# A mixture of experts with the slot lists made by products of one-hot matrices and the rows gathered for each tile

## The chip, the cores and the metric

The kernel runs on one core of one Trainium2 chip. The time is the device time of one execution in microseconds; a median over runs is quoted, and a profile is one execution of its own. PE is the matrix engine, DVE the vector engine, ACT the scalar engine, POOL the general engine, SP the engine that only issues transfers.

## The reference

Two pre-norm blocks on `x` of 2 x 1024 tokens with 256 features, all in float32: ALiBi attention with 32 heads, a mixture of experts, an RWKV-7 time mixing, and a feed-forward switched between two experts. The change lies in the second, which is

```
xf = layernorm(x)
gates = softmax(xf @ router_w.T)                  # 8 experts
topv, topi = top_k(gates, 2)
masked = zeros_like(gates) with topv at topi;  masked /= masked.sum() + 1e-20
for e in range(8):
    routed += (silu(xf @ wg[e]) * (xf @ wu[e]) @ wd[e]) * masked[:, e]   # hidden 176
shared = silu(xf @ sg) * (xf @ su) @ sd                                  # hidden 352
x = x + routed + shared
```

## The kernel before

The program is a row of blocks; at the end of a block all engines meet. Tokens lie 128 to a partition tile, 16 tiles (`TILES`), and four tiles make a chunk of 512 tokens (`TB`, four chunks, `NB`). A token chooses two experts, so there are 4096 choices (`CHOICES`). The kernel doesn't run each expert over all tokens: it sorts the choices by expert into slots, 128 slots to a tile, each expert's part rounded up to whole tiles. This gives at most 39 tiles (`SLOT_TILES`), and all 39 are worked on.

The blocks around the change, in order:

- `attention_phase` (L486). In the last but one of its units SP also issues one transfer of 5 MB that fills the slot table in memory with blank rows (`slot_rows`, `blank`), and waits for it at the end of the phase (L721 to L724, L761).
- `project_attention` (L764), beside which SP loads all weights of the mixture, and `layernorm_stats` (L66).
- `normalise_rows` (L902). DVE normalises the 16 tiles into `rows`, which holds each row twice (once for each choice) with two more words for the choice's number and its gate; POOL makes the second copy (L923). PE turns the tiles and ACT takes them into `xt`.
- `route_and_share` (L946). PE forms the router's logits (L1012) and turns them to token order (L1016). DVE has a chain of some 30 small operations, each waiting for the one before (`c.link`): softmax, the two picks, the mask, the gates; PE sums the mask over tokens (L1024, L1025), and DVE makes from it the slot of each choice, `at32` (L1116), and the expert of each tile, `tile_expert` (L1121). POOL then scatters the rows to the slot table with 32 indirect transfers of 128 rows (L1133) and waits until all have landed. Beside this the shared expert runs in 12 steps, three for a chunk: `gate_and_up(i)` on PE (L997), the silu on ACT (L1045), the product `share(i)` on DVE (L1071), `down(i)` on PE (L1006); after three steps DVE adds the chunk to `x` (`take(n)`, L1076).
- `routed_experts` (L1138). PE first loads the 39 expert numbers into registers, one by one (`value_load`). Then for each tile j: SP loads the slots (L1174; five buffers, `RING_T`), PE turns them (L1196), gate and up product with that expert's weights, addressed by the register (L1204), silu on ACT (L1251), product on DVE (L1276), PE turns it (L1213), down product (L1221), DVE weighs it with the gate (L1284), POOL scatters the result to `moe_chosen` by the choice's number (L1308). A slot buffer is loaded again when its tile's scatter has landed, for the gate and the number are read from it. At the end SP loads the results back by chunk, two for each token, and DVE adds them to `x` (L1298) and takes the statistics for the next normalisation (L63).

SP's queue holds the slot loads and, after the sixth, 16 loads of weights for the time mixing.

## Time and profile before

| | |
|---|---|
| median of 3 runs | 1524.67 us (1517.23 to 1526.18) |
| profiled execution, its time | 1534.31 us |
| its span | 1532.5 us |
| busy PE, DVE, ACT, POOL | 1253.8, 866.6, 565.9, 246.1 us |
| mean granted clock of TensorE | 0.924 of full speed |
| moved by DMA | 56.71 MB, mean 37 GB/s |

The span is the time from the first to the last instruction; the time of an execution holds a little more. A time in a timeline counts from the span's start. "Idle before" is how long the engine had nothing to do ahead of that work, and the name behind the arrow is what ended it: another engine's instruction, a DMA, "issue" when nothing that the profile shows was waited for, "remote" when the signal came from nothing recorded on this core. A clock of 1.00 is 2.4 GHz and 0.50 is 1.2 GHz.

### The profile page before, as it was taken

To read this page: it belongs to the slowest core of one execution; us is meant where nothing else is said; L and a number is where in the kernel's file an instruction comes from. 1 tells how busy PE (TensorE), PEld (TensorE's weight loads), DVE (VectorE), ACT (ScalarE), POOL (GpSimd) and SP (SyncE) were. 2 spreads that over 40 slices of the span, in tenths; PEclk is the share of its full clock that TensorE was granted. 3 is DMA by queue.
4 is the path that set the end of the run, shared out by engine and by line. 5 is a ranking of instruction groups with operands and counts; after the bars stand their busy time and mean duration, and the time that the engine had idled before them with its cause. 6 is when DMAs were issued, how large, how long until landed. Compare 5 with 4: busy or idle time off the path is not lost. (4 is left out here: it accounts for less than half of the span.)

```text
span 1532.5 us, 32535 instructions
## 1 busy us (share of the span) xinstructions
PE 1253.8 (82%) x12936; PEld 710.8 (46%) x12968; DVE 866.6 (57%) x1704; ACT 565.9 (37%) x846; POOL 246.1 (16%) x454
## 2 busy tenths in 40 slices
PE   5779999999999997947366662877599999976998
PEld 3423333333333335524244441333288888864665
DVE  5477888888888844401011226777667766665122
ACT  2417777777777773300122221533221112102211
POOL 3310000001001004360012220122232112100000
PEclk9959999999999998888689995999899999998999
DMA  3401112211211324020122223000020000000000
GB/s 110 67 3 25 26 26 39 32 25 29 42 24 25 93 70 142 20 91 18 50 71 61 66 63 110 0 1 0 1 72 3 4 4 4 4 2 0 14 14 28
DMA packets 42589, 56.71 MB, mean 37 GB/s; under 512 B 13067, under 2 KB 32235, under 8 KB 42123
## 3 DMA queue, kind: packets, MB, share of 16 engines
q1 hardware_dynamic: 38299, 44.67, 12.5%
q0 software_dynamic: 3408, 9.34, 1.7%
q8 instruction: 86, 1.41, 0.4%
q10 hardware_dynamic: 768, 1.05, 0.2%
q14 instruction: 28, 0.23, 0.1%
HBM read 28.73 MB, written 16.59 MB: 30 GB/s over the span
## 5 line engine op out<-in xcount | busy, mean ns | idle before, releaser
L664 DVE TENSOR_REDUCE at_block_max<-at_p_ring 128x4 f32<-128x512 f32 x576 | 367.6, 685 | 75.9 <-PE at_p_ring L570 41.6
L641 ACT ACTIVATE at_probs<-at_p_score,abias 128x1024 f32<-128x1024 f32 (+2 forms) x320 | 318.9, 1029 | 122.6 <-PE at_p_score L600 68.4
L570 PE MATMUL at_p_ring<-kt,qt 64*128 64x128 bf16 (+3 forms) x1152 | 186.9, 284 | 18.5 <-PEq L730 7.3
L615 PE MATMUL at_p_out<-at_probs,at_vs 128*32 128x512 f32 (+3 forms) x1536 | 164.2, 500 | 0.4 <-ACT at_probs L641 0.4
L594 PE MATMUL at_p_score<-qt,kt 64*128 64x512 bf16 (+3 forms) x768 | 145.9, 331 | 5.7 <-ACT at_probs L641 4.8
L570 PEld LDWEIGHTS at_p_ring<-kt,qt 64*128 64x128 bf16 x1152 | 69.9, 96 | 130.2 <-DVE at_block_max L664 86.3
L1276 DVE TENSOR_TENSOR ex_hidden<-ex_p_gu,ex_act 128x176 f32<-128x176 f32 x39 | 13.3, 341 | 140.2 <-ACT ex_act L1251 140.2
L1196 PE MATMUL ex_p_turn<-ident,ex_slot 128*128 128x128 f32 x78 | 17.6, 313 | 76.3 <-DMA ex_slot<-moe_slots 49.3
L594 PEld LDWEIGHTS at_p_score<-qt,kt 64*128 64x128 bf16 x768 | 38.3, 94 | 86.2 <-ACT at_probs L641 55.2
L707 POOL TENSOR_TENSOR at_shift<-shift,at_row_max 128x16 f32<-128x16 f32 x32 | 7.1, 220 | 422.8 <-DVE at_row_max L670 422.8
L1308 POOL DMA_INDIRECT moe_chosen<-ex_y,ex_slot x39 | 37.2, 955 | 196.2 <-DVE ex_y L1284 195.6
L1970 ACT COPY rc_ta<-rc_bank 128x256 f32<-128x256 f32 x32 | 10.3, 375 | 149.2 <-PE rc_bank L1741 149.2
L1388 DVE SCALAR_TENSOR_TENSOR tm_xm<-tm_xx,vec,xt_mix 128x512 f32<-128x512 f32 x48 | 44.5, 974 | 35.4 <-PE tm_p_full L1498 30.0
L2210 DVE SCALAR_TENSOR_TENSOR x<-ff_p_out,branch,x 128x256 f32<-128x256 f32 x32 | 13.3, 477 | 87.2 <-PE ff_p_out L2166 87.2
L600 PE MATMUL at_p_score<-anticausal,ident 128*128 128x128 bf16 (+1 forms) x384 | 62.3, 244 | 0.0
L2175 PE MATMUL ff_p_in<-xt_ffn,w_in 128*128 128x512 f32 x128 | 61.3, 607 | 1.2 <-PEq L2100 1.2
L1204 PE MATMUL ex_p_gu<-w_routed,ex_xs 128*128 x156 | 60.2, 514 | 0.1
L2166 PE MATMUL ff_p_out<-w_back,ff_hidden 128*128 128x256 f32 x256 | 59.8, 379 | 0.0
L1245 ACT COPY ex_xs<-ex_p_turn 128x256 f32<-128x256 f32 x39 | 14.5, 372 | 117.8 <-PE ex_p_turn L1196 117.8
L2166 PEld LDWEIGHTS ff_p_out<-w_back,ff_hidden 128*128 128x128 f32 x256 | 48.6, 190 | 18.6 <-issue 13.4
L2190 ACT ACTIVATE ff_hidden<-ff_p_in,b_in 128x512 f32<-128x512 f32 x32 | 22.0, 688 | 86.2 <-PE ff_p_in L2175 86.2
L615 PEld LDWEIGHTS at_p_out<-at_probs,at_vs 128*32 128x32 f32 x1536 | 30.2, 108 | 45.6 <-issue 38.1
(301 smaller groups left out, 2220.2 us busy)
## 6 DMA issues: line engine op xcount, KB each, us to landing
qt<-qparts SPq DMA_DIRECT2D x96, 64.0 KB, 2.4
kt<-kparts SPq DMA_DIRECT2D x96, 64.0 KB, 2.4
moe_slots<-in_blank_dram SPq DMA_DIRECT2D x1, 5031.0 KB, 19.3
ex_slot<-moe_slots SPq DMA_DIRECT2D x39, 129.0 KB, 2.1
ex_back<-moe_chosen SPq DMA_DIRECT2D x8, 512.0 KB, 5.0
w_routed<-in_w_routed_dram SPq DMA_DIRECT2D x1, 2816.0 KB
x<-in_x_dram SPq DMA_DIRECT2D x4, 512.0 KB, 8.4
out_dram<-x SPq DMA_DIRECT2D x4, 512.0 KB, 2.9
```

Source lines behind the costliest of these rows:

```text
L570: mm = pe.matmul(bank[:, col:col + nb * P], qt[nxt][h * ROWS:(h + 1) * ROWS, pair, t * P:(t + 1) * P], kt[nxt][h * ROWS:(h + 1) * ROWS, pa ...
L594: mm = pe.matmul(score[:, h, i * w:(i + 1) * w], kt[now][h * ROWS:(h + 1) * ROWS, pair, key * P:(key + 1) * P], qt[now][h * ROWS:(h + 1) * ...
L600: mm = pe.matmul(over, ident16[:, :], anticausal16[:, 0:len(pairs), :], start=False, stop=True, skip_group_check=True)
L615: mm = pe.matmul(p_out[32 * h:32 * h + 32, left(k):QC], vs[(now - e[2]) % BUFS][:, key, h, :], probs[g % PROBS][:, h % 2, at:at + w], star ...
L641: act.activation(probs[g % PROBS][:, :, 0:len(pairs) * w], p_score[g % 2][:, :, 0:len(pairs) * w], ACT.Exp, bias=abias[:, c * TPB + key:c ...
L664: dve.tensor_reduce(dst, src, AX.X, ALU.max).then_inc(s["fill_used"], 1)
L1204: mm = pe.matmul(p_gu[j % 2][:, 0:2 * HIDDEN], xs[j % 2][:, h, :], w_routed[:, h, ds(expert[j], 1), :].rearrange("p a c -> p (a c)"), star ...
L1308: pool.indirect_dma_start(chosen_out[:, :], bass.IndirectOffsetOnAxis(ap=slot[i][:, AT_ID:AT_ID + 1].bitcast(I32), axis=0), y[i][:, :], No ...
L1388: ins = dve.scalar_tensor_tensor(xm[i % 2][:, h, :], xx[:, h, :], v_("x_" + MIXES[i], h), xt[:, h, ds(m, 1), 1:].rearrange("p n c -> p (n ...
L2166: mm = pe.matmul(p_out[e][:, t, :], hidden[m % 2][:, t * P:(t + 1) * P], w_out[:, m, :], start=m % FT == 0 and t % 2 == 0, stop=m % FT == ...
L2175: mm = pe.matmul(p_in[m % 2][:, :], w_in[:, h, m * P:(m + 1) * P], xt[:, h, ds(n, 1), 1:].rearrange("p n c -> p (n c)"), start=h == 0, sto ...
L2190: act.activation(hidden[m % 2][:, :], p_in[m % 2][:, :], ACT.Gelu if m < FT else ACT.Relu, bias=b_in[:, m:m + 1]).then_inc(hidden_ready, 1)
```

## The change

`route_and_share` and `routed_experts` become one block, `mixture`.

- The slot table in memory, its blank fill and the 32 scatters go. Instead SP stores the normalised rows once, in token order, as `table` (four transfers of 512 KB from `normalise_rows`). `rows` holds each row once, without the two words.
- Which choice lies in a slot is found by products. For each choice DVE splits its slot into tile (`at_tile`) and lane (`at_lane`). `heat(k)` makes, for the first or the second choices of all tokens, a one-hot matrix of the lane (16 x 128 for each partition), one of the tile (16 x 40), and the latter times the choice's number and times its gate. PE multiplies the lane matrix with the values (`invert(k)`, 16 products each), and the sum over 32 products holds for each slot its choice's number and gate. From it DVE makes `source32`, the row to be read, and `target32`, the row to be written; an empty slot reads a valid row and writes to a row of its own behind the results.
- A tile's rows are fetched from `table` by an indirect transfer of POOL, `gather(j)`. POOL's order is: eight gathers, then for each tile the scatter of its result and the gather for the tile eight further. Slots and results have eight buffers each (`SLOTS`); a semaphore serves two neighbouring tiles, and PE waits for a pair.
- The expert numbers of eight tiles are packed in one word, three bits each; PE loads five words and takes the numbers out by shift and mask.
- The shared expert: steps 0 to 5 run beside the lists, `gate_and_up(0)` now ahead of the turn of the logits; step 6 to 11 behind the tiles, beside the loads of the results and their additions (`add_back`).
- SP issues the 16 weight loads when eight tiles are turned, and loads the results back with one transfer for each chunk, not two.

```diff
@@ normalise_rows
+            @block.sync
+            def _(sp):
+                for n in range(NB):
+                    sp.wait_ge(xn_ready, 4 * n + 4)
+                    sp.dma_start(table[n * TB:(n + 1) * TB, :].rearrange("(p t) e -> p t e", t=TB // P),
+                                 rows[:, 4 * n:4 * n + 4, :]).then_inc(table_stored, 16)
-                    pool.tensor_copy(rows[:, t, 1, 0:E], rows[:, t, 0, 0:E])
@@ mixture, tensor
+                def invert(k):
+                    pe.wait_ge(hot_ready, k + 1)
+                    for t in range(k * TILES, (k + 1) * TILES):
+                        mm = pe.matmul(p_map[:, 0:2 * PLACED], hot_lane[:, t, :], hot_value[:, t, :, :].rearrange("p v j -> p (v j)"),
+                                       start=t == 0, stop=t == TOPK * TILES - 1)
+                    mm.then_inc(map_ready, 1)
+                def turn(j):
+                    if j % 2 == 0:
+                        pe.wait_ge(pair_sem(gathered, j), pair_count(j))
...
                 mm.then_inc(logits_ready, 1)
+                pe.wait_ge(moe_loaded, moe_count * 16)
+                gate_and_up(0)
                 pe.wait_ge(logits_in, 1)
...
                 down(0)
-                for i in range(2, len(STEPS_S)):
+                gate_and_up(2)
+                down(1)
+                gate_and_up(3)
+                down(2)
+                invert(0)
+                invert(1)
+                gate_and_up(4)
+                down(3)
+                gate_and_up(5)
+                down(4)
+                down(5)
+                pe.wait_ge(mapped, 1)
+                words = [pe.value_load(word32[0:1, w:w + 1], min_val=0, max_val=EXPERTS ** PER_WORD - 1) for w in range(WORDS)]
+                number = [(words[j // PER_WORD] >> (3 * (j % PER_WORD))) & (EXPERTS - 1) for j in ALL]
+                pe.wait_ge(down_used, 2)
+                turn(0)
+                turn(1)
+                expert_gate_and_up(0)
+                for j in ALL:
+                    if j + 2 < SLOT_TILES:
+                        turn(j + 2)
+                    if j + 1 < SLOT_TILES:
+                        expert_gate_and_up(j + 1)
+                    turn_hidden(j)
+                    if j >= 1:
+                        expert_down(j - 1)
+                expert_down(SLOT_TILES - 1)
+                gate_and_up(FIRST_SHARED)
+                pe.wait_ge(y_ready, SLOT_TILES)
+                for i in range(FIRST_SHARED + 1, len(STEPS_S)):
                     gate_and_up(i)
                     down(i - 1)
@@ mixture, vector
+                def heat(k):
+                    part = slice(k * TILES, (k + 1) * TILES)
+                    each = [P, TILES, PLACED]
+                    mark = c.mark(dve.tensor_tensor(hot_tile[:, part, :], at_tile[:, k, :].unsqueeze(2).to_broadcast(each),
+                                                    route[:, ROUTE["number"]].unsqueeze(1).to_broadcast(each), ALU.is_equal))
+                    c.mark(dve.tensor_tensor(hot_lane[:, part, :], at_lane[:, k, :].unsqueeze(2).to_broadcast([P, TILES, P]),
+                                             route[:, ROUTE["lanes"]].unsqueeze(1).to_broadcast([P, TILES, P]), ALU.is_equal))
...
+                share(1)
+                heat(0)
+                share(2)
+                heat(1)
+                share(3)
...
+                take(0)
+                dve.wait_ge(map_ready, 2)
...
+                dve.sem_inc(mapped, 1)
+                share(4)
+                share(5)
+                take(1)
...
+                share(6)
+                share(7)
+                add_back(0)
+                share(8)
+                take(2)
+                add_back(1)
+                share(9)
+                block_stats(0)
+                share(10)
+                block_stats(1)
+                share(11)
+                add_back(2)
+                block_stats(2)
+                add_back(3)
+                take(3)
+                dve.wait_ge(down_used, NB)
+                block_stats(3)
@@ mixture, gpsimd
+                def gather(j):
+                    pool.indirect_dma_start(slot[j % SLOTS], None, table[:, :],
+                                            bass.IndirectOffsetOnAxis(ap=source32[:, j:j + 1], axis=0)).then_inc(pair_sem(gathered, j), 16)
+                pool.wait_ge(table_stored, NB * 16)
+                pool.wait_ge(mapped, 1)
+                for j in range(SLOTS):
+                    gather(j)
                 for j in ALL:
                     pool.wait_ge(y_ready, j + 1)
+                    pool.indirect_dma_start(chosen_out[:, :], bass.IndirectOffsetOnAxis(ap=target32[:, j:j + 1], axis=0),
+                                            y[j % SLOTS], None).then_inc(pair_sem(y_stored, j), 16)
+                    if j + SLOTS < SLOT_TILES:
+                        pool.wait_ge(turned, j + 1)
+                        gather(j + SLOTS)
```

## Rows read from the trace of the kernel before

**Rows 1.** Table of stretches: length, busy us of each engine, clock, DMA share, GB/s.
```profile
619.30:671.50 52.20, 48.05 (x148) 24.08 (x148) 16.31 (x46) 8.46 (x13) 21.72 (x23) 0.97 0.15 55
671.50:691.00 19.50, 0.55 (x2) 0.00 (x0) 2.51 (x3) 1.19 (x2) 9.17 (x10) 0.60 0.20 72
691.00:721.50 30.50, 26.89 (x80) 16.05 (x80) 5.11 (x6) 2.38 (x4) 0.00 (x0) 0.92 0.00 1
721.50:747.00 25.50, 0.00 (x0) 0.00 (x0) 0.00 (x0) 0.00 (x0) 0.00 (x0) 0.53 0.09 26
747.00:914.60 167.60, 118.13 (x468) 78.59 (x468) 31.67 (x78) 38.09 (x117) 35.33 (x37) 0.91 0.23 69
914.60:939.90 25.30, 0.00 (x0) 0.00 (x0) 15.70 (x25) 0.01 (x1) 1.92 (x2) 0.56 0.55 181
```

**Rows 2.** Timeline, 684 to 692 us: start, duration, work, idle time before it and releaser.
```profile
684.07 0.60 ACT L1045 ACTIVATE ro_act<-ro_bank 128x512 f32<-128x512 f32 x1 [23.44 <-remote]
688.30 1.53 DVE L1071 TENSOR_TENSOR ro_hidden<-ro_bank,ro_act 128x512 f32<-128x512 f32 x2 [25.85 <-remote]
...
691.10 3.75 PE L1006 MATMUL ro_p_down<-w_shared,ro_hidden 128*128 128x256 f32 x8 [19.05 <-DVE x L1076]
```

**Rows 3.** POOL's indirect DMAs by line: min/median/max ns, starts, time to landing.
```profile
L1133 POOL DMA_INDIRECT moe_slots<-rows,ro_at x32: 956/960/1166, 643.1 to 682.4; - x32
...
L1308 POOL DMA_INDIRECT moe_chosen<-ex_y,ex_slot x39: 954/954/961, 755.7 to 915.9; - x39
...
DMA to landing us min/median/max: 2.4/2.4/4.0
```

**Rows 4.** Timeline of PE at the first tiles.
```profile
747.04 1.11 PE L1196 MATMUL ex_p_turn<-ident,ex_slot 128*128 128x128 f32 x4 [27.04 <-issue]
...
753.62 0.38 PE L1213 MATMUL ex_p_hidden<-ident,ex_hidden 128*88 128x128 f32 x2
...
756.11 0.38 PE L1213 MATMUL ex_p_hidden<-ident,ex_hidden 128*88 128x128 f32 x2
```

**Rows 5.** Waits in the tiles (747 to 914.6 us): total us, times, longest.
```profile
PE ex_p_turn L1196 <- DMA ex_slot<-moe_slots: 49.3, 28, 5.2
```

**Rows 6.** The page's list of DMA issues: times issued, KB, us to landing.
```profile
moe_slots<-in_blank_dram SPq DMA_DIRECT2D x1, 5031.0 KB, 19.3
```

**Rows 7.** Timeline of the router and the lists.
```profile
619.35 7.03 PE L1012 MATMUL ro_bank<-xt_moe,w_router 128*8 128x512 f32 x16 [0.95 <-PEq L910]
...
628.48 1.06 PEld L1016 LDWEIGHTS ro_bank<-ident,ro_logits_t 8*128 8x128 f32 x16 [3.02 <-ACT ro_logits_t L1036]
...
629.66 0.29 DVE L1079 TENSOR_REDUCE ro_top<-ro_bank 128x16 f32<-128x128 f32 x1 [11.97 <-PE ro_bank L1016]
...
635.15 0.38 DVE L1088 TENSOR_TENSOR ro_mask<-ro_pick 128x128 f32<-128x128 f32 x1
...
642.61 0.18 DVE L1116 CAST ro_at<-ro_at 128x32 int32<-128x32 f32 x1
...
645.56 3.60 PE L997 MATMUL ro_bank<-xt_moe,w_in_shared 128*128 128x512 f32 x8
648.99 1.89 PE L1006 MATMUL ro_p_down<-w_shared,ro_hidden 96*128 96x256 f32 x8
650.72 3.60 PE L997 MATMUL ro_bank<-xt_moe,w_in_shared 128*128 128x512 f32 x8
```

**Rows 8.** Groups of DVE instructions, 610 to 945 us: count, busy us, mean ns.
```profile
L1076 DVE TENSOR_TENSOR x<-ro_p_down,x 128x1024 f32<-128x1024 f32 x4 | 4.9, 1217 | 2.8 <-PE ro_p_down L1006 2.8
...
L1118 DVE TENSOR_TENSOR ro_past<-route,ro_upto 128x312 f32<-128x312 f32 x1 | 0.5, 472 | 0.0
```

**Rows 9.** Timeline at the end of the tiles.
```profile
912.67 1.89 PE L1221 MATMUL ex_p_y<-w_down,ex_hidden_t 88*128 x8
...
915.93 0.96 POOL L1308 DMA_INDIRECT moe_chosen<-ex_y,ex_slot  x1 [0.30 <-issue]
...
923.75 1.22 DVE L1298 TENSOR_TENSOR x<-ex_back,x 128x1024 f32<-128x1024 f32 x1 [8.67 <-DMA ex_back<-moe_chosen]
```

More of the change, by code:

```diff
@@ L943, in _, with mixture @@
                              p_turn[j % 4][:, :].rearrange("p (h c) -> p h c", h=EH)).then_inc(taken, 1)
-def route_and_share(nc, x, xt, wr, ident, priority, route, before, ones, rows, slots, tile_expert, w_in, w_shared,
-                    moe_loaded, moe_count):
+def mixture(nc, x, xt, wr, ident, priority, route, before, ones, rows, table, table_stored, chosen_out, w_in, w_shared, w_routed, w_down,
+            stats, moe_loaded, moe_count, loaded, pairs):
+    SLOTS, PAIRS = 8, 4
     with ExitStack() as ctx:
@@ new lines, in mixture @@
+        pair_gate, at, at_tile, at_lane = (sb(n, K3) for n in "pair_gate at at_tile at_lane".split())
+        at32, tile32, lane32 = (sb(n, K3, I32) for n in "at32 tile32 lane32".split())
+        past, expert = sb("past", [P, PLACED, EXPERTS]), sb("expert", [P, PLACED])
+        packing, word, word32 = sb("packing", [P, PLACED]), sb("word", [P, WORDS]), sb("word32", [P, WORDS], I32)
+        slot_of, empty, target, source = sb("slot_of", [P, 2, PLACED]), sb("empty", [P, PLACED]), sb("target", [P, PLACED]), sb("source", [P, PLACED])
@@ new lines, in mixture @@
+        p_gu, p_hidden, p_turn = bank[0:2], bank[2:4], bank[4:6]
+        p_y = [p_down[:, 0, :], p_down[:, 2, :]]
+        (chain_s, logits_ready, logits_in, tok_ready, softmax, mask_ready, ranks_ready, hot_ready, map_ready, mapped,
+         gate_ready, up_ready, s_act_ready, s_hidden_ready, down_ready, down_used,
+         turned, taken, gu_ready, act_ready, hidden_ready, hidden_turned, hidden_taken, y_summed, y_ready) = (
+            sem(n) for n in "chain logits_ready logits_in tok_ready softmax mask_ready ranks_ready hot_ready map_ready mapped "
+            "gate_ready up_ready s_act_ready s_hidden_ready down_ready down_used "
+            "turned taken gu_ready act_ready hidden_ready hidden_turned hidden_taken y_summed y_ready".split())
@@ new lines, in _ @@
+                act.activation(work["gate"][:, :, :], work["shifted"][:, :, :], ACT.Exp).then_inc(softmax, 1)
+                for i in range(FIRST_SHARED):
+                    share_silu(i)
+                take(0)
+                take(1)
+                silu(0)
+                for j in ALL:
+                    if j + 2 < SLOT_TILES:
+                        take(j + 2)
+                    if j + 1 < SLOT_TILES:
+                        silu(j + 1)
+                    take_hidden(j)
+                for i in range(FIRST_SHARED, len(STEPS_S)):
+                    share_silu(i)
@@ L2313, in two_blocks_program @@
             xt = sb0("xt_moe", [P, EH, NB, TB + 1])
-            rows = sb0("rows", [P, TILES, TOPK, ROW])
-            normalise_rows(nc, x, mean, rstd, ident, xt, rows, route)
-            route_and_share(nc, x, xt, w_router, ident, priority, route, before, ones, rows, slots, tile_expert, w_in_shared, w_shared,
-                            moe_loaded, len(moe_pairs))
+            rows = sb0("rows", [P, TILES, E])
+            normalise_rows(nc, x, mean, rstd, ident, xt, rows, table, table_stored)
             mix_pairs = [
@@ L2323, in two_blocks_program @@
                 (level1_t[:, :], d["level1_t"]), (eye[:, :], d["eye"])]
-            routed_experts(nc, x, ident, slots, chosen_out, tile_expert, w_routed, w_down, stats, mix_loaded, mix_pairs)
+            mixture(nc, x, xt, w_router, ident, priority, route, before, ones, rows, table, table_stored, chosen_out, w_in_shared, w_shared,
+                    w_routed, w_down, stats, moe_loaded, len(moe_pairs), mix_loaded, mix_pairs)
         data = {n: sb(n, [P, EH, NB, TB]) for n in "rt at bt kt vt gt bonus".split()}
@@ L2377, in shape_constants @@
         head_ones=row // RN == col // RN, priority=np.tile(EXPERTS - np.arange(EXPERTS), (P, 1)),
-        route=route, blank=blank, before=row < col, ones=np.ones((P, P)),
+        route=route, before=row < col, ones=np.ones((P, P)),
         head_spread=p[:, None, None] == 32 * np.arange(2 * EH)[:, None] + p // RN, head_columns=p[:, None] // RN == np.arange(32)[None],
```

414 lines of the change are left out of this document (182 added, 232 removed).

## The prediction

> **What bounds the kernel now.** First the page's list of slices and its critical chain: the chain holds only the last feed-forward phase, so the stretch between the attention and the time mixing, where this change lies, is to be read from the trace itself. Then the table of stretches [rows 1]. From the router (619.3 us) to the end of the mixture (939.9) are 320.6 us, in which PE works 193.6, DVE 71.3, ACT 50.1. Five losses are seen. (1) From 671.5 to 691.0 PE works 0.55 us; ACT and DVE stand for 23.4 and 25.9 us and for that the profile names nothing on this core, and PE then waits for DVE [rows 2]. This falls into the 40 us in which POOL issues 32 scatters back to back; ACT starts again 1.6 us after the last of them began [rows 2, 3]. (2) From 691.0 to 721.5 the rest of the shared expert runs on PE; the tiles can't begin before it. (3) From 721.5 to 747.0 no engine works: PE loads the 39 expert numbers, 27.0 us of "issue", 0.65 us each. (4) The tiles take 167.6 us, 4.3 us each; PE works 118.1 us of it. Two tiles that wait for nothing follow each other by 756.11 - 753.62 = 2.49 us [rows 4]; the others wait for their slots' load, 49.3 us in 28 waits [rows 5], and PE's clock is 0.91 for it. (5) From 914.6 the sums come back from memory: 25.3 us with PE idle. PE is the engine that ends each stretch when nothing holds it, so I cost the change as a new timetable for it and for DVE, which makes the lists.
>
> **Up to the router.** The blank fill of 5 MB goes. It took 19.3 us to land [rows 6], SP issued it in the last but one unit of the attention and nobody waited for it before the end of that phase: nothing. If it took bandwidth from the key stacks, a microsecond is gained. POOL's copy of the rows in `normalise_rows` goes; it ended beside ACT's last copies, so nothing. Four stores of the rows come onto SP, issued while DVE normalises; they have some 40 us before the first gather: nothing, at worst the 0.5 us of an issue.
>
> **Lists.** `gate_and_up(0)` moves ahead of the 16 small transposes. A `gate_and_up` and `down` pair takes 650.72 - 645.56 = 5.16 us, of which 3.43 are the first. The router's products end at 626.4, so the transposes start at 629.8, not 628.48, and DVE's chain at 630.9, not 629.66 [rows 7]. From there DVE works without a gap: softmax and picks 5.9 us as before (635.15 + 0.38 - 629.66), mask at 636.8; from the mask to the places 7.3 (642.79 - 635.53, share(0) in it), and four more small operations of 0.18 and a gap, 0.85, which split tile and lane: 644.9. Then share(1) and `heat`. A DVE operation costs 0.47 us for 312 elements a partition and 1.22 for 1024 [rows 8]: 1.05 ns for each between, so 0.69 for a share's 512, 0.82 for 640 and 2.3 for 2048. `heat` has three of 640 and one of 2048: 4.75 us. share(1), two heats, share(2) and share(3) end at 656.5. Expert numbers and words are six operations (1.9), take(0) one (1.2), and eight small ones (1.75) make the map: `mapped` at 661.4. PE is beside this: it runs shares 1 to 3 between the lists; the 16 products of `invert` are 32 passes, no row shows their shape; between 0.07 us (the 8-column transposes) and 0.45 us (a 512-column pass) each; I take 0.15, near the first, for 80 columns are few. Only the second half, 2.4 us, can be late, and DVE's packing covers it; at 0.45 it would cost 3.
>
> PE then still has gate_and_up(4), down(3), gate_and_up(5), down(4), down(5): 658.5 + 3.4 + 1.7 + 3.4 + 1.7 + 1.7 = 670.4, and take(1) ends at 671.7. Behind it the five words are loaded: 5 x 0.65 = 3.3. The first turn is at 675. The eight first gathers (8 x 1.26 = 10 us) start at 661.7 and are hidden under the shares. **675.0 against 747.0: 72 us less.** In it are the 19.5 us of the standstill, 22 of the 25.5, and the 30.5 of the shared expert, half of which stood behind the lists.
>
> How the numbers are taken out of the words is not in the trace: two register operations (shift, mask) for a tile, or for each of its four uses. From below nothing: a free tile keeps PE's 2.49 us although its products already take their address from a register [rows 4]. From above 0.65 us each, which is a load from memory [rows 4]. I take nothing.
>
> **Tiles.** Before, a scatter had to land and the slot be loaded again (ring of five), 21 us for five tiles. Now gather and result have eight buffers each. The way round: result to scatter 0.3, POOL 0.96 + 0.3 + 0.96, landing 2.4 [rows 3], the partner of the pair 2.5, and three tiles until the next result 7.5 to 9: 16.5 us in eight tiles of 2.49 = 19.9. So landings may be 3.4 us later than they were before they tell. Next late is POOL: two indirect DMAs for a tile, 0.96 + 0.30 each, as in the scatter run (32 in 40.5 us) [rows 2, 3]: 2.52, just over PE's 2.49. A gather is not in the trace. Below, it costs a scatter's 0.96; nothing in a descriptor list of 128 rows of 1 KB says less. Above, I double it, for it reads memory at scattered places. I take 0.96, plus a little for its two waits: 2.6 a tile, 101 us, and 3 us to fill: 675 to 779. **104 against 167.6: 63.5 us less.** POOL's gather stands behind `y_ready` of its tile, and the next scatter behind the gather; both only matter if POOL is the slower one. SP's 16 loads of mixing weights come earlier but no longer stand before the slots on the same queue.
>
> **Behind the tiles.** Six shares on PE at 5.16 us are 31 us. The last scatter is issued 1.3 us after PE's last down product, and the first addition follows 7.8 us after that (923.75 - 915.93) [rows 9], in the cover of shares 6 and 7. By the written order, T being the end of the tiles on PE: share(8) T + 13.4, take(2) T + 20.2, add_back(1) T + 22.7, share(9) 23.4, down(9) 25.2, gate_and_up(11) 28.6, down(11) 32.2; DVE has add_back(2) until 32.5, four statistics 1.5, add_back(3) 2.4, take(3) 1.2 and the last four statistics 1.5: **T + 39.5 against 25.3: 14.2 more.**
>
> **The sum.** 72 + 63.5 - 14.2 = 121 us. The profiled execution's 1534.3 us (span 1532.5) would be 1413; it lies 0.6% over the median of the runs, 1524.67, from which the same 121 make 1404. Behind the mixture nothing changes.
>
> **The rivals.** A measurement of this kernel can't tell 1% (15 us) from no change.
>
> *B, the gathers are dear.* At twice a scatter's 0.96 POOL needs 3.5 us a tile, 0.9 over my 2.6: 35 us, 1439; from 1.3 us on it shows. For it: reads at scattered places, no row. Against it: POOL's time hardly moved between scatters to two tensors (954 and 960 ns) [rows 3].
>
> *C, the standstill comes back.* While POOL issues without a break ACT and DVE stop: 19.5 us lost in 40. With 98 us of such issue that would be 46 us: 1450. For it is rows 2; against it, that a stopped PE stops POOL as well, because a scatter waits for its result, and that the first 20 us of the scatters passed unharmed. In the Trainium skill, "DMA: Bandwidth & Descriptors", section "Queues, rings and completion order", each DMA engine takes its queue rows in turn, packet by packet. By that rule a stream on one row can't hold up another's fetches, and this rival would cost nothing; the 25.9 us of rows 2 neither show nor refute it, for their cause has no row.
>
> *D, DVE locks POOL out.* If each of DVE's two operations in a tile stopped POOL's descriptors, their 31.67 / 39 = 0.81 us [rows 1] would come on top of 2.52: 3.33 a tile, 28 us over my stage, 1432. Against it: 39 issues beside those very operations took 954 to 961 ns [rows 3]. The Trainium skill states such an exclusive lock in "SBUF — State Buffer", section "Who interferes with whom", for DVE's two-port modes; by it this rival would be the forecast, if DVE's operations here are in such a mode.
>
> *E, slower than before.* The unpacking is done again at each of the four uses, eight register operations in a tile on PE's queue beside its 24 instructions (16 weight loads and the 16 small products beside them took 1.06 us, 0.033 each [rows 7], so 0.8). The change loses if a tile takes over (104 + 121) / 39 = 5.8 us, thus from 0.62 us an operation on; at 0.65, the price of a word's load, a tile takes 6.0 us and the kernel 1537. Against it: addresses are worked out for eight passes of a tile already, inside 2.49 us.
>
> *F, the ring doesn't do what it says:* gathers land so late that tiles keep the 4.3 us of before: 64 us, 1467.
>
> **Chances.** A, the forecast, 1390 to 1425: 0.68. B, 1415 to 1440: 0.12. C, 1425 to 1460: 0.10. D, 1425 to 1440: 0.04. E 0.03. F 0.03. From 1390 to 1440 lie A but for a sliver, B and D, about 0.8. The lower end is the tile at 2.49 us (4 us less) and DVE's chain some 8 us shorter; the upper is B at a doubled gather. Only E is slower by over 1%, A to D and F are faster by more; 0.01 is left for within 1%.
>
> **What would show it.** In the profile after: the first turn near 675 us with at most 5 us of PE idle before it; POOL's gathers near 0.96 us, tiles 2.5 to 2.6 us apart and PE waiting for gathers in fewer than 5 of 39; no standstill of ACT and DVE without a named releaser; PE's clock at 1.0 (2.4 GHz) through tiles and late shares; 39 to 40 us from the last tile's down product to the first operation of the next normalisation. It is wrong if POOL is busy without a gap and PE waits at each turn (B, D), if all engines stop together (C), or if PE's idle time before its products is named "issue" (E).

## The result, and the profile after

The changed kernel takes 1400.8 us (median; 1400.2 to 1407.0 in 4 runs) against 1525.35 us: a ratio of 0.920, 95% interval 0.916 to 0.924. Its profiled execution took 1400.6 us, span 1398.7, mean clock 0.952. The forecast was 1404. The profiled execution of the kernel before took 1534.3 us, so between the two profiles lie 133.7 us, where 121 were forecast; the last section but two says where the 12 more come from.

Table of stretches of the changed kernel (router to first tile, tiles, tail), with length, busy time of each engine, clock and DMA share, the counterpart of [rows 1]:

```profile
618.96:672.20 53.24, 49.38 (x197) 28.63 (x197) 29.07 (x70) 8.35 (x13) 7.81 (x8) 0.97 0.07 20
672.20:773.40 101.20, 100.28 (x469) 73.08 (x470) 31.71 (x77) 37.41 (x117) 66.75 (x68) 0.98 0.36 110
773.40:812.10 38.70, 31.25 (x97) 17.35 (x95) 21.92 (x33) 3.58 (x7) 1.95 (x2) 0.98 0.32 119
```

PE is busy 181 of 193 us, where it was busy 194 of 321. In the tiles it has no gap to speak of, and in the tail, where it stood idle for 25 us, it now works 31 of 39.

Timeline of the changed kernel from the lists to the first tile (DVE's tile and lane numbers, a one-hot of 2048, the products, the map's last operation, the first gathers, PE's first turn), to be held against [rows 3, 4, 7]:

```profile
643.40 0.17 DVE L1307 CAST ro_at_lane<-ro_lane 128x32 f32<-128x32 int32 x1
...
644.95 2.29 DVE L1245 TENSOR_TENSOR ro_space<-ro_at_lane,route 128x2048 f32<-128x2048 f32 x1
...
651.52 7.27 PE L1059 MATMUL ro_bank<-ro_hot_value,ro_space 128*128 128x80 f32 x64
...
660.32 0.18 DVE L1330 TENSOR_SCALAR ro_source<-ro_row 128x40 int32<-128x40 int32 x1
...
661.44 1.16 POOL L1363 DMA_INDIRECT ro_space<-moe_table,ro_source  x1 [56.30 <-DVEq L1331]
662.90 0.95 POOL L1363 DMA_INDIRECT ro_space<-moe_table,ro_source  x1 [0.30 <-issue]
...
672.20 0.66 PE L1069 MATMUL ro_bank<-ident,ro_space 128*128 128x128 f32 x4 [1.32 <-DVE x L1225]
```

The map is ready at 660.5 and the first turn comes 11.7 us later, behind the shared expert's step 5. What ends PE's wait of 1.32 us is `take(1)`; no time named "issue" stands before PE's turn, so the five word loads cost nothing that can be seen. At 0.65 us each they need 3.3 us, so at least 2 us of them were done while the shared expert's last down product still ran.

Two tiles on PE and on POOL in the changed kernel, and the groups of POOL in the tiles (count, busy us, mean ns, idle before):

```profile
684.27 0.38 PE L1086 MATMUL ro_bank<-ident,ro_e_hidden 128*88 128x128 f32 x2
684.49 1.03 PE L1094 MATMUL ro_p_down<-w_down,ro_hidden_t 88*128 x4
...
686.76 0.38 PE L1086 MATMUL ro_bank<-ident,ro_e_hidden 128*88 128x128 f32 x2
```

```profile
683.92 1.00 POOL L1372 DMA_INDIRECT moe_chosen<-ro_space,ro_target  x1 [0.30 <-DVE ro_space L1238]
685.23 0.97 POOL L1363 DMA_INDIRECT ro_space<-moe_table,ro_source  x1 [0.30 <-issue]
686.50 1.00 POOL L1372 DMA_INDIRECT moe_chosen<-ro_space,ro_target  x1 [0.30 <-issue]
```

```profile
L1372 POOL DMA_INDIRECT moe_chosen<-ro_space,ro_target x39 | 38.6, 989 | 26.3 <-DVE ro_space L1238 16.8 <-issue 9.4
L1363 POOL DMA_INDIRECT ro_space<-moe_table,ro_source x31 | 30.1, 972 | 9.4 <-issue 8.2 <-PE ro_bank L1069 1.2
```

PE's pitch is 686.76 - 684.27 = 2.49 us, the free tile of [rows 4]; POOL's is 2.58. The list of PE's waits in the tiles has 0.5 us for gathers in two waits, where [rows 5] has 49.3 in 28, and no wait of any engine names "remote":

```profile
PE ro_bank L1069 <- DMA ro_space<-moe_table,ro_source: 0.5, 2, 0.3
```

DVE's last work in the tail of the changed kernel; PE's last down product ends at 805.6:

```profile
802.84 2.47 DVE L1261 TENSOR_TENSOR x<-rows,x 128x1024 f32<-128x1024 f32 x2
805.34 1.41 DVE L63 BATCH_NORM_STATS2 stats<-x 128x6 f32<-128x256 f32 x4
806.66 2.46 DVE L1261 TENSOR_TENSOR x<-rows,x 128x1024 f32<-128x1024 f32 x2
809.16 1.23 DVE L1225 TENSOR_TENSOR x<-ro_p_down,x 128x1024 f32<-128x1024 f32 x1
```

For all kernels of this study, from their profiles (us): when the first tile is turned, from there to the issue of the last scatter, from that to the next normalisation (ACT's table load), the rest, and the span. The router starts between 615.9 and 620.3 in all but "no scatters", where it starts at 627.5. Counted from its own router's start, the first turn comes 127.7 us later in the first profile of before, and 110.0 in the second, with the ring of eight and without scatters.

| kernel | first turn | tiles | tail | rest | span |
|---|---|---|---|---|---|
| before | 747.0 | 168.9 | 24.0 | 592.6 | 1532.5 |
| before, second profile | 730.3 | 177.3 | 24.6 | 588.1 | 1520.2 |
| words | 705.6 | 188.5 | 24.6 | 588.3 | 1507.0 |
| ring of eight | 729.0 | 112.0 | 24.6 | 588.3 | 1453.8 |
| ring of eight and words | 708.9 | 112.2 | 25.0 | 592.5 | 1438.6 |
| the same, mixing loads last | 708.1 | 103.0 | 24.3 | 588.4 | 1423.8 |
| no scatters | 737.6 | 181.0 | 24.5 | 587.7 | 1530.8 |
| changed, all shared steps first | 710.0 | 104.2 | 23.0 | 590.3 | 1427.4 |
| changed | 672.2 | 102.6 | 37.3 | 586.6 | 1398.7 |
| changed, second profile | 672.5 | 100.7 | 37.3 | 592.5 | 1403.0 |
| changed, gathers doubled | 672.4 | 138.4 | 37.3 | 588.1 | 1436.1 |
| changed, ring of six | 672.2 | 169.9 | 37.3 | 587.4 | 1466.8 |
| changed, ring of six, own signals | 672.3 | 109.6 | 37.3 | 590.6 | 1409.8 |
| changed, other tail | 672.6 | 102.9 | 33.2 | 590.3 | 1399.0 |

The column "rest" varies by 6 us between two profiles of one kernel: the 6 us that the changed kernel seemed to gain behind the mixture are no part of the change.

### The profile page after: what moved, and what is told of

It reads as the page before. It is cut to its first block and busy times, and to the rows that moved or that the text cites. A ratio compares the mean times of both kernels' runs of the same rounds, so it can differ in the third digit from the quotient of the medians.

```text
span 1398.7 us, 32573 instructions
## 1 busy us (share of the span) xinstructions
PE 1239.6 (89%) x13000; PEld 708.0 (51%) x13032; DVE 877.0 (63%) x1727; ACT 564.4 (40%) x846; POOL 248.2 (18%) x444
## 3 DMA queue, kind: packets, MB, share of 16 engines
q1 hardware_dynamic: 29499, 36.55, 11.7%
## 5 line engine op out<-in xcount | busy, mean ns | idle before, releaser
L2232 PEld LDWEIGHTS ff_p_out<-w_back,ff_hidden 128*128 128x128 f32 x256 | 48.6, 190 | 18.6 <-issue 13.4
L1077 PE MATMUL ro_bank<-w_routed,ro_xs 128*128 x156 | 54.4, 472 | 0.4 <-ACT ro_xs L1162 0.4
L1363 POOL DMA_INDIRECT ro_space<-moe_table,ro_source x39 | 38.0, 973 | 67.9 <-DVEq L1331 56.3
L1807 PE MATMUL rc_bank<-rc_X,rc_ab 64*64 64x64 f32 x1280 | 46.7, 219 | 2.8 <-DVE rc_X L1953 1.5
L1231 DVE TENSOR_TENSOR ro_e_hidden<-ro_bank,ro_e_act 128x176 f32<-128x176 f32 x39 | 13.3, 342 | 54.0 <-ACT ro_e_act L1168 54.0
L600 PEld LDWEIGHTS at_p_score<-anticausal,ident 128*128 128x128 bf16 x384 | 21.9, 97 | 48.9 <-issue 45.7
```

The source lines that it names most:

```text
L600: mm = pe.matmul(over, ident16[:, :], anticausal16[:, 0:len(pairs), :], start=False, stop=True, skip_group_check=True)
L1077: mm = pe.matmul(p_gu[j % 2][:, 0:2 * HIDDEN], xs[j % 2][:, h, :], w_routed[:, h, ds(number[j], 1), :].rearrange("p a c -> p (a c)"), star ...
L1363: pool.indirect_dma_start(slot[j % SLOTS], None, table[:, :], bass.IndirectOffsetOnAxis(ap=source32[:, j:j + 1], axis=0)).then_inc(pair_se ...
L1807: mm = pe.matmul(bank[b][r, n, h * width:(h + 1) * width], lhs(b, r, h, half, par), rhs(b, r, h), start=True, stop=True, skip_group_check= ...
L2232: mm = pe.matmul(p_out[e][:, t, :], hidden[m % 2][:, t * P:(t + 1) * P], w_out[:, m, :], start=m % FT == 0 and t % 2 == 0, stop=m % FT == ...
```

## The experiments

The theory was the prediction's: PE's timetable bounds all stretches; the parts of the gain are the ring (a slot's way round), the words, and PE's work in place of idle time. The rivals were B to F, and that the 19.5 us standstill (PE, ACT and DVE stopped together in the first profile of before, loss 1 of the prediction) belongs to the scatters. "Us less" and "us slower" are worked out from the ratios, for each run was taken beside runs of the kernel before; "..." in a code cut stands for lines left out.

### The parts, made alone in the kernel before

**Ring of eight.**

```diff
-    RING_T = 5
+    RING_T, PAIRS = 8, 4
...
-                    pe.wait_ge(slot_loaded[j % RING_T], (j // RING_T + 1) * 16)
+                    if j % 2 == 0:
+                        pe.wait_ge(pair_sem(slot_loaded, j), pair_count(j))
```

> The kernel before with slot and result rings of eight (as the change has), the slot loads left with SP; a semaphore serves two neighbouring tiles. The prediction's reason (a slot's way round, 21 us for five tiles, sets the 4.3 us of a tile): eight tiles in the same 21 us are 2.6 us each, so the tiles take 101 to 104 us and the kernel is 62 to 67 us faster. Rival (a tile needs something that the indirect gather alone gives, because the slot loads on SP's queue or the table's memory traffic are the limit): pitch stays above 3.3 us, less than 40 us gained. Rival (the ring isn't the cause at all): no change.

Measured: 1456.5 us, ratio 0.958 (0.954 to 0.962), 64 us less. The ring is half of the whole gain, and it needs neither gathers nor new lists. The tiles took 112 us, though, not 101 to 104: one turn waits 7.8 us for its slot, of which the fourth experiment below has the cause.

**Five words.**

```diff
-                expert = [pe.value_load(tile_expert[0:1, j:j + 1], min_val=0, max_val=EXPERTS - 1) for j in ALL]
+                words = [pe.value_load(tile_expert[0:1, w:w + 1], min_val=0, max_val=EXPERTS ** PER_WORD - 1) for w in range(WORDS)]
+                expert = [(words[j // PER_WORD] >> (3 * (j % PER_WORD))) & (EXPERTS - 1) for j in ALL]
```

> The kernel before with the expert numbers of eight tiles packed in one word: PE loads five words, not 39 numbers, and takes the numbers out by shift and mask. By the prediction 27.0 us of loads become 5 x 0.65 = 3.3: 22 to 24 us faster. Rival E (unpacking is paid at each of the four uses of a tile): here a tile of 4.3 us has 1.8 us of slack on PE, so up to 0.2 us an operation would be hidden, and beyond that the tiles' stretch is longer than 168 us. Rival (something else, such as the slots' loads, ends the wait ahead of the first tile): under 15 us gained.

Measured: 1511.0 us, ratio 0.992 (0.989 to 0.995), 12 us by the ratio and 10 by the medians, half of what was expected. The loads shrank nearly as worked out; these two lines are the lists of waits of the second profile of before and of this kernel:

```profile
PE ex_p_turn L1196 <- issue: 27.0, 1, 27.0
```

```profile
PE ex_p_turn L1203 <- issue: 5.1, 1, 5.1
```

34 loads fewer save 21.9 us, 0.64 each, so some 1.9 us of the wait aren't loads.

The other half was lost in the tiles. Stretches from the first turn to the last scatter, of before's second profile and of this kernel:

```profile
730.30:907.50 177.20, 124.63 (x468) 82.38 (x468) 32.20 (x78) 38.44 (x117) 36.42 (x38) 0.87 0.22 66
```

```profile
705.60:894.10 188.50, 134.39 (x468) 87.21 (x468) 32.18 (x78) 38.89 (x117) 36.49 (x39) 0.83 0.21 62
```

The waits for slots are nearly the same (51.1 and 52.0 us); PE's own 468 products took 10 us longer, at a clock of 0.83, not 0.87. The first profile of before had 118 us at 0.91. So the 11 us between these two profiles go with PE's slower products, in a ring where PE's work is inside the way round. That is one profile each; that the clock is the cause and not a companion of the waits, and why it lay lower here, wasn't tested.

**Both.** The edit is the sum of the two.

> The kernel before with both parts: rings of eight, and the expert numbers in five words. The ring alone gave 64.6 us (1456.5), the words alone 10 us (1511.0), though their first tile began 22 us earlier: their tiles took 187 us where those of before took 168. If the words' gain was eaten by the ring of five (a slot's way round holds the tiles, and the clock stays at 0.85), with eight buffers the whole 22 us are seen: 1433 to 1438. Rival E (a tile pays for the unpacking on PE's queue): the tiles' pitch goes above 2.55 us and the kernel stands at 1443 to 1448.

Measured: 1439.0 us, ratio 0.946 (0.942 to 0.950): 18 us on top of the ring, of the 22 expected; 1 us above the range of the first theory and 4 below that of the second. The first turn lies 20 us earlier than with the ring alone and the tiles are as long, so a tile doesn't pay for the unpacking. Rival E falls here, as it does by the pitch of 2.49 us.

**The mixing weights out of the slots' way.** In the kernel with both parts SP's queue holds the 16 loads between two slot loads, and PE then waits; two views, SP's and PE's timeline:

```profile
731.87 0.43 SPq L1188 DMA_DIRECT2D eye<-in_eye_dram  x1
732.35 1.38 SPq L1185 DMA_DIRECT2D ex_slot<-moe_slots  x3
```

```profile
735.26 0.69 PE L1209 MATMUL ex_p_turn<-ident,ex_slot 128*128 128x128 f32 x2 [7.54 <-DMA ex_slot<-moe_slots]
```

```diff
-                    if j == RING_T:
+                    if j == SLOT_TILES - 1:
                         for dst, src in pairs:
```

> The kernel before with rings of eight and five words, and the 16 loads of mixing weights issued behind the last slot load instead of behind the ninth. In that kernel's trace SP's queue issued them from 724.0 to 732.4 us and PE then waited 7.5 us for a slot; without them in the way a tile keeps 2.49 us and the kernel is 7 to 9 us faster than with both parts: 1430 to 1432, ratio 0.940. Rival (a tile waits there for a slot anyway, or the weights now come too late for the time mixing): no change.

Measured: 1427.0 us, ratio 0.938 (0.935 to 0.942), 12 us less than with both parts, where 7 to 9 were expected: 9 in the tiles, as their column shows, and the remainder within what "rest" varies by. In the change the slots come by POOL, so these loads stand before nobody.

### The standstill

**No scatters.**

```diff
                 pool.wait_ge(placed, 1)
-                for t in range(TILES):
-                    for k in range(TOPK):
-                        pool.indirect_dma_start(slots[:, :], bass.IndirectOffsetOnAxis(ap=at32[:, k, t:t + 1], axis=0),
-                                                rows[:, t, k, :], None).then_inc(scattered, 16)
-                pool.wait_ge(scattered, TILES * TOPK * 16)
```

> The kernel before without its 32 scatters; this leaves out the placing of the rows, so the tiles work on blank rows, and the results are read back from the rows behind the choices. Two kernels that hold the same scatters showed no standstill. If it is an accident of single executions, this kernel shows none either and stands within 4 us of the kernel before (1515 to 1521). If the scatters bring it about in some executions and in others not, half of it or more is gained on the median: 8 to 20 us. The tiles are at 4.3 us either way.

Measured: 1523.7 us, ratio 1.001 (0.998 to 1.004): the 32 scatters cost nothing on the median, where 8 to 20 us were expected if they brought the standstill about often. Its profile has none.

**Before again.** No edit.

> The kernel before once more, for a second profile. The first profile had a standstill of 19 us that three kernels with the same router and scatters did not have, and a tiles' stretch of 168 us, where two others with the ring of five had 181 and 187. If the standstill is an accident of single executions, it is absent here; if the tiles' stretch varies by execution, it is anywhere from 168 to 188 here, and the span follows from the two: about 1513 us with the first profile's tiles, up to 1532 with the slower ones.

Measured: 1522.0 us, span 1520.2. At the place where ACT had stood 23.4 us in [rows 2], this second profile of the same kernel has

```profile
680.41 0.59 ACT L1045 ACTIVATE ro_act<-ro_bank 96x512 f32<-96x512 f32 x1 [8.50 <-PE ro_bank L997]
685.57 0.60 ACT L1045 ACTIVATE ro_act<-ro_bank 128x512 f32<-128x512 f32 x1 [4.57 <-PE ro_bank L997]
```

No standstill, with all 32 scatters running. Of the six profiles that hold these scatters one has it, and there it moved the first turn by 17.7 us (127.7 against 110.0 from the router). It is an accident of that execution and worth nothing on the median; what stopped the engines in it stays open, and so does whether the scatters had a part in it. That profile had another deviation, the other way: tiles of 168.9 us, where three others with the ring of five have 177 to 189. In the span the one takes back half of the other: 16.7 us more ahead of the first turn, 8.4 less in the tiles, 0.6 less in the tail, 4.5 more in "rest", 12.3 more in all.

### What half of the shared expert behind the tiles is worth

```diff
-    FIRST_SHARED = 2 * SHARED_MT
+    FIRST_SHARED = NB * SHARED_MT
...
```

Steps 6 to 11 then run ahead of the first turn, and DVE's products and `take(2)`, `take(3)` with them.

> The changed kernel with all twelve steps of the shared expert ahead of the tiles. By the prediction's working six steps of 5.16 us stand ahead of the first turn (31 us more) and the tail shrinks from 38.8 to the 25.3 us of before, in which PE idles: 17 to 18 us slower, 1416 to 1420. Rival (the late half isn't worth it, because the additions behind it are delayed or because the early half was hidden anyway): within 4 us of the changed kernel.

Measured: 1424.3 us, ratio 0.937 (0.933 to 0.941): 25 us slower than the changed kernel, where 17 to 18 were expected. The tail shrinks by 14.3 us, near the 13.5 worked out. The first turn, though, is 37.8 us later, not 31. PE's timeline in this kernel says why:

```profile
698.15 2.44 PE L1052 MATMUL ro_p_down<-w_shared,ro_s_hidden 128*128 128x256 f32 x8 [2.01 <-DVE x L1220]
700.38 4.86 PE L1043 MATMUL ro_bank<-xt_moe,w_in_shared 128*96 128x512 f32 x8
705.08 3.62 PE L1052 MATMUL ro_p_down<-w_shared,ro_s_hidden 128*128 128x256 f32 x16
710.01 0.66 PE L1069 MATMUL ro_bank<-ident,ro_space 128*128 128x128 f32 x4 [1.32 <-DVE x L1220]
```

Its stretch from 699.5 to 702.9 us, with PE's clock as the last figure but two:

```profile
699.50:702.90 3.40, 3.40 (x6) 1.47 (x5) 0.00 (x0) 0.00 (x0) 0.00 (x0) 0.50 0.02 5
```

Twice (680.4 and 698.2 us) the first down product of a chunk waits 2.0 us for DVE's `take`, and behind the second such wait, at a granted clock of 0.50 (1.2 GHz), a product group that takes 3.60 us elsewhere takes 4.86. Ahead of the tiles the six steps don't cost 5.16 us each but 6.3.

The comparison with the kernel "mixing loads last" is the instructive one. Both have the ring, the words and all shared steps first; one places rows by 32 scatters, the other by products and gathers. 1427.0 and 1424.3 us, 0.938 and 0.937: no difference. First turns at 708.1 and 710.0, tiles 103.0 and 104.2. With the shared expert in front the scatters were hidden. The lists by products only pay because their map is ready at 660.5, which lets the tiles begin at 672 and the six steps go to the tail. The scatters ended at 683.4 [rows 3], and with a landing (2.4) and a slot's load (2.3) the first slots would be there at 688: by this estimate the deferral with scattered lists would begin its tiles some 16 us later than the changed kernel. That kernel wasn't tried, so how the last 26 us (1427.0 against 1400.8) split between the deferral and the lists isn't shown. The parts add up: ring 64, words 18, loads of the mixing weights 12, lists and deferral together 26, in all 120 of the 121 us.

### POOL and the ring

**Gathers doubled.**

```diff
+                    if j >= SLOTS:
+                        n = j - SLOTS
+                        if n >= 2:
+                            pool.wait_ge(spare_loaded[n % 2], n // 2 * 16)
+                        pool.indirect_dma_start(spare_slot[n % 2][:, :], None, table[:, :],
+                                                bass.IndirectOffsetOnAxis(ap=source32[:, j:j + 1], axis=0)).then_inc(spare_loaded[n % 2], 16)
```

> The changed kernel with each of the 31 later gathers issued twice, the second into a spare buffer: three indirect transfers of POOL for a tile. If POOL's issuing is what comes next behind PE (2.57 us of POOL against 2.49 of PE), a tile takes 3 x 1.27 = 3.8 us and the kernel is 31 x 1.3 = 40 us slower, 1436 to 1445. If only PE counts and POOL's queue has slack that its busy time doesn't show, under 10 us. If POOL's unbroken issuing stops ACT and DVE (rival C), gaps of 10 us and more that name no releaser appear and it is above 1455. DVE's two operations in a tile (rival D) would show in indirect transfers above 1.2 us.

Measured: 1437.8 us, ratio 0.946 (0.942 to 0.950), 39 us slower than the changed kernel (37 by the medians, 36 in the tiles of the profiles). POOL's timeline in this kernel:

```profile
742.64 0.99 POOL L1379 DMA_INDIRECT moe_chosen<-ro_space,ro_target  x1 [0.30 <-issue]
743.93 0.97 POOL L1364 DMA_INDIRECT ro_space<-moe_table,ro_source  x1 [0.30 <-issue]
745.21 0.95 POOL L1370 DMA_INDIRECT ro_spare_slot<-moe_table,ro_source  x1 [0.30 <-issue]
746.46 0.99 POOL L1379 DMA_INDIRECT moe_chosen<-ro_space,ro_target  x1 [0.30 <-DVE ro_space L1239]
```

3.82 us a tile on POOL. So POOL is what comes next behind PE, and rival B's way of pricing holds: it had 35 us for 3.5 us of POOL a tile, and 3.82 cost 36 to 39. With POOL issuing without a break neither a standstill (C) nor a longer issue beside DVE's operations (D) appears; its 109 indirect transfers took 0.94 to 1.00 us, but for the first, 1.16. The lock of the Trainium skill's "SBUF — State Buffer", section "Who interferes with whom", is thus not seen with DVE's operations of these tiles; the page ties it to some of DVE's modes and operands, and no run shows whether any operation here is in such a mode.

**Ring of six.**

```diff
-    SLOTS, PAIRS = 8, 4
+    SLOTS, PAIRS = 6, 3
```

> The changed kernel with six gather and six result buffers (three pairs), not eight. The prediction's way round of 16.5 us (result, POOL's queue, landing, partner, three tiles) in six tiles gives 2.75 us a tile: 31 x 0.2, some 6 to 10 us slower, with waits for gathers in every second tile. Rival (the way round is shorter than 14.9 us, so that six are enough): no change. Rival (landings of gathers are far later than the scatters' 2.4 us): 20 us and more.

Measured: 1468.7 us, ratio 0.965 (0.962 to 0.968): 68 us slower, a clear miss: 6 to 10 were expected. In size it fits the rival that gathers land late, but they land 2.8 us after issue (median), 2.9 in the change. PE's timeline of one period:

```profile
726.84 0.44 PE L1069 MATMUL ro_bank<-ident,ro_space 128*128 128x128 f32 x2 [2.46 <-DMA ro_space<-moe_table,ro_source]
...
729.61 0.39 PE L1069 MATMUL ro_bank<-ident,ro_space 128*128 128x128 f32 x2
...
735.16 0.44 PE L1069 MATMUL ro_bank<-ident,ro_space 128*128 128x128 f32 x2 [2.90 <-DMA ro_space<-moe_table,ro_source]
```

This pair takes 8.3 us, not 5.0; the pairs of the whole stretch take 8.7 on average (169.9 us for 19.5 of them), with PE's clock at 0.87. I had treated the way round as a constant, 16.5 us, to be divided by six. But PE works in order: between the turn of tile j and its down product stand the turns of later tiles, and if these wait, the way round is longer. With a signal for a pair, two pair periods q pass from the turn of an even tile to the turn behind which its partner's down product stands, and from there to the next use of the two buffers PE's own work, DVE, POOL and landing take 8.2 us: 2q + 8.2. (I had split them into 2.3 of PE and 5.9 of the others; in these rows it is nearer 3.0 and 5.3.) Three pairs must cover it: q = 8.2. This sum was made with the trace of six at hand, so the fit is no test; the next run is one. With four pairs, q = 4.1 would do, and PE needs 4.98: free, with a reserve of 1.8 us on the way round (4 x 4.98 - 2 x 4.98 - 8.2), not 3.4.

**Ring of six, a signal for each tile.** The counting says that not the buffers but the pair is dear.

```diff
-                    if j % 2 == 0:
-                        pe.wait_ge(pair_sem(gathered, j), pair_count(j))
+                    pe.wait_ge(gathered[j % SLOTS], (j // SLOTS + 1) * 16)
```

> The ring of six again, but PE waits for each tile's own gather and not for a pair's. From the first trace of six: a pair takes q = 8.3 us, and the way from the turn of an even tile to its buffers being filled again is two pair periods (the turns of the next two pairs stand in it, with their waits) plus 2.3 us of PE's own work and 5.9 us of DVE, POOL and landing: 2q + 8.2 = 3q gives q = 8.2, which is what was measured. With a signal for each tile the same way is 3p + 8.2 = 6p: p = 2.73 us a tile, so the tiles take some 107 to 112 us, not 169, and the kernel stands at 1405 to 1415. Rival (six buffers are too few by themselves, whoever waits): within 10 us of 1469.

Measured: 1410.5 us, ratio 0.926 (0.921 to 0.931), 58 us faster than the same six buffers with pairs, and the tiles take 109.6 us, inside the 107 to 112 forecast before the run. PE's waits for gathers with pairs and with a signal for each tile:

```profile
PE ro_bank L1069 <- DMA ro_space<-moe_table,ro_source: 43.2, 16, 5.3
```

```profile
PE ro_bank L1068 <- DMA ro_space<-moe_table,ro_source: 3.4, 5, 2.1
```

The same counting gives the ring of five, afterwards: 3p + 2.3 + 0.9 + 0.3 + 0.96 + 2.4 + 2.3 (slot load) = 5p, p = 4.6 us, where its tiles have 4.3 to 4.8.

### The change's own order, again and altered

**The changed kernel again.** No edit.

> The changed kernel itself on the same chip as its parts: ratio 0.920 as before, the tiles 101 us, and the time behind the mixture (from the first operation of the third normalisation to the end) tells whether the 6 us that it lost between the two first profiles come back (592.6 before, 586.6 after): if it is the change that shortens it, again 586 to 587; if it varies from execution to execution, anything from 586 to 593, in this and in the other kernels of this call.

Measured: 1399.4 us, ratio 0.919 (0.915 to 0.924), tiles 100.7 us, rest 592.5 us: the rest varies from execution to execution.

**Another tail.** DVE adds and measures each chunk as its results come:

```diff
                 add_back(0)
                 share(8)
-                take(2)
                 add_back(1)
-                share(9)
                 block_stats(0)
-                share(10)
+                take(2)
+                share(9)
                 block_stats(1)
-                share(11)
                 add_back(2)
-                block_stats(2)
+                share(10)
                 add_back(3)
+                block_stats(2)
+                share(11)
                 take(3)
```

> The changed kernel with another order of DVE's work behind the tiles: the additions and statistics of a chunk come as soon as its results are there, between the products of the late steps, and only take(3) and the statistics of the last chunk stand behind PE's last down product. In the trace of the changed kernel DVE works on add_back(3) and take(3) until 4.7 us after that product's end; with the new order 2.4 us of addition and 1.5 of statistics come earlier: 2 to 4 us faster, 1396 to 1398. Rival (the late shares wait longer for their products, because DVE is late with them): no gain or up to 3 us slower.

In its trace only `take(3)` and the last statistics stand behind PE, and the tail is 33.2 us, not 37.3:

```profile
803.04 0.67 DVE L1220 TENSOR_TENSOR ro_s_hidden<-ro_bank,ro_s_act 96x512 f32<-96x512 f32 x1
805.80 1.22 DVE L1225 TENSOR_TENSOR x<-ro_p_down,x 128x1024 f32<-128x1024 f32 x1 [2.09 <-PE ro_p_down L1052]
807.05 1.41 DVE L63 BATCH_NORM_STATS2 stats<-x 128x6 f32<-128x256 f32 x4
```

The time, 1398.3 us, ratio 0.919 (0.916 to 0.922), can't be told from the changed kernel's: 4 us are less than what executions differ by. Its profile supports it; the measured time neither confirms nor refutes it.

## Why the prediction was right, step by step

The sum, 121 us less than before's median, gave 1404; measured 1400.8. The mechanism, PE's timetable, held; that the number came within 4 us is in part luck. Against the second profile of before, which has no standstill, 1522.0 - 1400.6 = 121.4, but made of other terms: first turn 58.1 (forecast 72), tiles 74.7 (63.5), tail 12.7 more (14.2). Against the first profile, from which the terms were taken, it is 133.7, and the forecast for it, 1413, missed by 12: each of the three stretches came out 1 to 3 us better than forecast, and "rest" gave 6.

- **Lists, 72 us less.** Against the first profile the first turn came 74.8 us earlier, against the second 58.1. Here one step failed in kind: the 19.5 us of the standstill were counted as a steady loss and are none (17.7 us in that one profile, nothing in the others). The chain itself held: DVE's tile and lane numbers ended at 643.6 (forecast 644.9), the map was ready at 660.5 (661.4), the last down product ended at 670.9 (670.4). The 3.3 us for five word loads don't show; the turn came at 672.2, not 675.0. Their price of 0.65 us was right, 0.64 in the kernel "words", though 27.0 / 39 would be 0.69: some 1.9 us of that wait aren't loads.
- **Products of `invert`, 0.15 us a pass.** 64 passes in 7.27 us, 0.11 each. The working halved the second part: 16 products are 32 passes, so 4.8 us by its own price, where it wrote 2.4; half of the measured 7.27 is 3.6. DVE waits 0.8 us for their end behind `take(0)`, and the map was still not late.
- **Tiles, 63.5 us less.** 168.9 became 102.6 in the first profile's terms, but the ring of five takes 177 us in the second profile and 181 in the one without scatters, so 75 is nearer. This mis-sizing (11 us) and what the standstill put into the lists' term (14 us too much in all) nearly cancel in the sum: it rested on one profile with one deviation up and one down. Nine of the 75 are the 16 weight loads that stood before slots; the prediction named them and gave them no price of their own.
- **The reason for the tiles' pitch.** Right in its result (PE's 2.49 with POOL just behind at 2.58, forecast 2.49 and 2.52), wrong in its working: the way round isn't 16.5 us in 19.9, but grows with the waits inside it, and the reserve is 1.8 us, not 3.4. At eight buffers that decides nothing; at six the signal for a pair costs 58 us.
- **Gather like a scatter, 0.96 us.** 0.97, landing 2.9 us after issue where a scatter's takes 2.4. The Trainium skill's fit in "DMA: Bandwidth & Descriptors", section "Anatomy of one DMA — SWDGE (gpsimd) path", 2.0 us plus bytes over 436 GB/s, gives as an estimate 2.3 us for these 128 KB: near the scatter, 0.6 short for the gather.
- **Tail, 14.2 us more.** 38.7 against 25.3, so 13.4. That the six steps are cheaper in the tail was in the sum, but not by how much: moved back to the front they cost 25 us, not 17 to 18, because there they also bring 4 us of waits for `take` and nearly 2 us of a lower clock.
- **Behind the mixture nothing.** Holds; the seeming 6 us came and went with the execution.
- **The rivals.** B: not dear, but POOL's time would have set the pitch as it says (36 to 39 us measured at 3.82 us a tile, 35 worked out at 3.5). C's price was 48 us by its own rates, not 46, and the chances add up to 1.00 without the last 0.01. C and D: nothing of them, even at three indirect transfers a tile. E and F: pitch 2.49 us. PE's clock in the tiles was 0.98, not 1.0.

## What to carry to other kernels

Before a loss in one profile becomes a term of a sum, look for it in a second profile of the same kernel: here one of 19.5 us with no named releaser was an accident, and another stretch erred by 8 us the other way. For a ring worked by an engine in order, count the way round in periods plus a constant and solve for the period; a signal shared by two tiles makes the period jump where the ring is just too short. And ask of a cheaper step what stands in front of it: the new lists with all of PE's shared steps still in front of the tiles took as long as the scattered ones, and what they are worth alone beside the deferral wasn't measured.

## What the hardware showed unexpectedly

- Register loads on PE's queue didn't show behind running matmuls: in the changed kernel five words, 3.3 us by [rows 4], added nothing, with PE idle for only 1.32 us ahead of the turn; with nothing running, 39 of them took 27.0 us and 5 took 5.1.
- In the tiles of the ring of five 468 products took 118.1 us at a granted clock of 0.91 (a mix of 2.4 and 1.2 GHz), 124.6 at 0.87 and 134.4 at 0.83, with 49 to 52 us of waits in each; the stretch went from 168.9 to 188.5 us. In the tiles of the changed kernel, where PE doesn't wait, the clock is 0.98 and the same products take 100.3 us. The ring of six with pairs shows the same: 126.1 us at 0.87. Here a ring that was too short cost its waits and slower products besides.
- Issuing without a break, POOL left 0.30 us between two indirect transfers, gather or scatter, and took 0.94 to 1.00 us for each (1.16 to 1.17 for the first in a kernel), also beside the DVE work of the tiles.
